# Who copies the turned tiles: ScalarE in place of VectorE, and a slot search in batches

## The chip, the core and the metric
The kernel runs on one core of a Trainium2 chip. The metric is the device time of one launch in microseconds (us), median over runs. TensorE multiplies and turns (transposes) tiles into PSUM, VectorE and ScalarE read PSUM and write SBUF, GpSimd issues the indirect DMAs (gather and scatter by row numbers), SyncE and ScalarE issue the plain DMAs. The engines run side by side, each in its own program order, and meet only at semaphores.

## The reference, cut to what matters
Images become patch tokens, text ids become rows of a table, and 12-head attention with its top 32 keys follows; all of that is unchanged here. The change is in the last step, a layer in which each of 2,176 tokens (32 sequences of 68) picks 4 of 128 matrices, twice: once to turn its 192 features into 128, once to turn 128 back into 192.

```
def topk_sparsify(weights, k):
    topk_vals, topk_idx = jax.lax.top_k(weights, k)
    ...
    sparse = sparse / (sparse.sum(axis=-1, keepdims=True) + 1e-08)
w_fk, _ = topk_sparsify(jax.nn.softmax(logits_fk, axis=-1), K)
w_rk, _ = topk_sparsify(jax.nn.softmax(logits_rk, axis=-1), K)
all_h = jnp.einsum('bsd,ndr->bsnr', x, neurons)
h = jnp.einsum('bsnr,bsn->bsr', all_h, weights)
all_out = jnp.einsum('bsr,nrd->bsnd', h, neurons)
out = jnp.einsum('bsnd,bsn->bsd', all_out, weights)
```

## The kernel before, in words
The tokens lie in NT = 17 tiles of 128, split into two parts: PARTS = tiles 0 to 8 and 9 to 16. The kernel doesn't form all 128 products of a token. It sends each token to the 4 matrices that it picked: every matrix has a block of HALVED = 64 slots in a part's slot table in DRAM, and tokens beyond 64 go to spill blocks behind the 128 own ones. Two matrices make one 128-slot tile, GROUP = 4 such tiles one group of 512 slots. Part 0 has 25 groups, part 1 has 24; 16 of each (PART_MAIN) hold the own blocks, the other 9 and 8 are spill groups, whose matrix is read from a table at run time. Part 0 takes its own groups first, part 1 its spill groups first (`first_order`).

The stages after the routing (which ends with `tiles_known`) are these.

- **Slot search** (`find_slots(r, i)` on VectorE, L1480 to L1507): for one tile i and one of the two products r, 12 instructions on 128x128 and 128x4 elements with a wait for the engine's own result between most of them give the 4 slot numbers of every token in `s_all`. `place` holds each token's position at each matrix, `base` where the matrix's spill begins. All 17 tiles of product 0 are searched first, in a row. Product 1's are searched one by one, each just before the tile's sum (`first_sums`).
- **Weights**: four small instructions on VectorE, after the 17 searches, then `weights_known`. `m_xT`, the buffer of turned tiles, lies over the first half of `place` and is cleared after that.
- **Send** (GpSimd, L692): four indirect DMAs for each tile write its rows to the slots `slots_x`, as soon as the tile's slots are known; `sent0` and `sent1` count them by part.
- **First product** (TensorE L1152 turns a slot tile, L1163 and L1166 multiply; 49 groups): SyncE loads groups of slot rows (`load_rows`, L456, 384 KB each, four buffers), TensorE turns them two tiles ahead (AHEAD = 2), VectorE copies the turned tile from PSUM to `m_halves` (L1534), TensorE multiplies, ScalarE copies the product to `m_yh` (L886) and stores a group (L889, 256 KB) to `slots_h`. SyncE's queue is in this order: the first 13 of 16 chunks of matrices, a wait for `weights_known` and `tiles_known`, the last 3 chunks (they lie over the routing's scratch), a wait for `sent0`, the row loads. The matrices of the second product (`load_r`, L462, 16 chunks of 768 KB) follow, chunk by chunk, as part 1's own groups free their room.
- **Gather, sum and spread**: when all of a part's first product is stored, GpSimd gathers for each tile the four rows of each token (`fetch(1, i)`, L700), VectorE sums them with the weights (`sum_back(1, i)`, L1559 and L1562), GpSimd scatters the sum to the 4 slots of the second product (`spread_sums`, L707). Its order is fetch(i), spread(i - 1), fetch(i + 1), with four gather buffers.
- **Second product** (L1201 turns, L1210 and L1212 multiply, VectorE copies at L1542, ScalarE keeps at L903): the same over `slots_g` and `slots_y`. It starts for a part when all of its sums are spread.
- **Output**: gathers from `slots_y` (L700 again), `sum_back(2, i)` with the residual (L1571), store (L487).

VectorE's order is written out by hand. It copies turned tiles group by group, and `beside` puts steps of other work between the groups: in the first product of part 1 the nine `first_sums` of part 0, in the second product of part 0 the eight of part 1, in the second product of part 1 the nine output sums of part 0. While VectorE searches and sums, no turned tile is copied.

## Time and profile before
| | |
|---|---|
| median of 3 runs | 1250.01 us (1247.91 to 1253.24) |
| profiled execution | 1248.79 us, span of its instructions 1247.0 us |
| mean granted clock of TensorE | 0.742 of full speed |
| busy in the span | TensorE 881.7 us, VectorE 753.1, GpSimd 529.8, ScalarE 329.2 |
| moved by DMA | 167.70 MB, mean 134 GB/s |

Times in the profile count from the span's start. The part before about 600 us is embedding, attention and routing, the part behind it the stages above. A row of the timeline gives start, length, engine, line, operation, output and input, how many instructions are merged, and in brackets the idle time before it with what ended it; "remote" is a releaser that the profile can't name. Each float32 matmul stands as two instructions.

### The profile page before, as it was taken

Reading aid. Unit: us, or ns where it says so; the run is one execution under the profiler, and the core shown is the slowest. Engines: PE = TensorE matmul, PEld = TensorE weight load, DVE = VectorE, ACT = ScalarE, POOL = GpSimd, SP = SyncE. Lnnn points to the kernel's source line nnn. Section 1 sums busy time; section 2 is a strip of 40 time slices with the busy share of each in tenths; the row PEclk is TensorE's granted clock in tenths of the full one; section 3 lists DMA queues with packets and bytes.
Section 4 is the critical chain, followed back from the end, with each engine's and each line's share of the span. In section 5 each row is a group of like instructions: output and inputs, shape, how many; then the busy total and the mean of one; then the engine's idle time right before and its main releaser. Section 6 shows DMA issues by size and latency. Waiting matters only on the chain.

```text
span 1247.0 us, 24432 instructions
## 1 busy us (share of the span) xinstructions
PE 881.7 (71%) x6616; PEld 750.0 (60%) x6616; DVE 753.1 (60%) x4773; ACT 329.2 (26%) x1042; POOL 529.8 (42%) x745
## 2 busy tenths in 40 slices
PE   4788988898989898667400099987778656757830
PEld 4788878888888787444200088987556333633630
DVE  1399999999999999444553444334445344424533
ACT  0234433333433343144200033211111222213410
POOL 3244444444544443245376500043443544454235
PEclk9778888787878655555555599987775676878975
DMA  5123332323233330086021555444785544447833
GB/s 189 33 69 110 141 110 89 109 89 109 90 109 111 113 113 25 19 208 162 7 79 67 169 196 188 149 126 126 256 318 205 182 146 151 140 154 229 272 127 95
DMA packets 81318, 167.70 MB, mean 134 GB/s; under 512 B 12944, under 2 KB 39376, under 8 KB 79536
## 3 DMA queue, kind: packets, MB, share of 16 engines
q1 hardware_dynamic: 55824, 111.18, 27.5%
q10 hardware_dynamic: 14112, 32.12, 7.4%
q0 software_dynamic: 11264, 23.09, 6.3%
q8 instruction: 42, 0.69, 0.2%
q14 instruction: 76, 0.62, 0.2%
HBM read 84.81 MB, written 81.53 MB: 133 GB/s over the span
## 4 chain that ended last, share of the span: by engine, by line
PE 36%; DVE 32%; issue 18%; POOL 5%; DMA 4%; another core or an unknown queue 2%; ACT 2%; DVEq 1%; SPq 0%; POOLq 0%; ACTq 0%
DVE work L1301 13%; DVE top L1295 9%; PE bank L1166 6%; PE bank L1163 5%; PE bank L1212 5%; PE bank L1152 4%; PE bank L1210 3%; POOL early L700 2%; PE bank L1201 2%; PE bank L1099 1%; PE bank L925 1%; PE bank L984 1%; PE bank L1006 1%; POOL slots_g L707 1%
## 5 line engine op out<-in xcount | busy, mean ns | idle before, releaser
L1301 DVE MATCH_REPLACE8 work<-top,work 102x68 f32<-102x68 f32 x1024 | 204.7, 212 | 0.0
L1534 DVE COPY place<-bank 96x256 f32<-96x256 f32 x196 | 74.5, 416 | 149.2 <-PE bank L1152 98.3
L1295 DVE MAX8 top<-work 102x8 f32<-102x68 f32 x1024 | 145.5, 213 | 3.2 <-ACT tru L767 1.9
L1152 PE MATMUL bank<-ident,early 128*96 128x128 f32 x392 | 73.4, 316 | 102.9 <-DMA early<-slots_x 101.2
L886 ACT ACTIVATE m_y<-bank 128x128 f32<-128x128 f32 x196 | 52.5, 278 | 304.2 <-PE bank L1166 207.9
L1542 DVE COPY place<-bank 128x128 f32<-128x128 f32 x196 | 47.5, 286 | 133.0 <-PE bank L1201 73.1
L707 POOL DMA_INDIRECT slots_g<-early,s_all x68 | 66.1, 973 | 138.8 <-DVE early L1562 123.2
L1152 PEld LDWEIGHTS bank<-ident,early 128*96 128x96 f32 x392 | 52.3, 175 | 118.3 <-issue 117.9
L700 POOL DMA_INDIRECT early<-slots_h,s_all x68 | 65.2, 959 | 122.9 <-DMA slots_h<-m_y 102.5
L925 PE MATMUL bank<-xa,early 128*96 128x144 f32 x512 | 102.0, 352 | 16.8 <-DVE early L1319 16.0
L903 ACT ACTIVATE m_y<-bank 128x192 f32<-128x192 f32 x196 | 61.1, 331 | 170.5 <-PE bank L1212 78.8
L1166 PE MATMUL bank<-f_all,place 96*64 96x128 f32 x1024 | 92.6, 324 | 15.0 <-issue 11.1
L925 PEld LDWEIGHTS bank<-xa,early 128*96 128x96 f32 x512 | 91.5, 200 | 18.2 <-issue 15.9
L1212 PE MATMUL bank<-r_all,place 128*64 128x192 f32 x512 | 70.3, 400 | 40.5 <-DVE place L1542 25.6
L700 POOL DMA_INDIRECT early<-slots_y,s_all x68 | 64.7, 952 | 68.8 <-DMA slots_y<-m_y 29.9
L1166 PEld LDWEIGHTS bank<-f_all,place 96*64 96x64 f32 x1024 | 71.9, 160 | 30.2 <-issue 18.2
L1006 PE MATMUL bank<-v,pT 68*68 68x17 f32 x768 | 75.9, 250 | 14.6 <-ACT pT L792 14.6
L1006 PEld LDWEIGHTS bank<-v,pT 68*68 68x68 f32 x768 | 74.0, 196 | 17.1 <-ACT pT L792 17.1
L692 POOL DMA_INDIRECT slots_x<-early,s_all x68 | 66.0, 970 | 40.8 <-DVE s_all L1506 20.6
L1163 PE MATMUL bank<-f_all,place 96*128 x544 | 73.5, 293 | 10.5 <-ACT m_y L886 4.3
L629 POOL TENSOR_TENSOR sc<-work,tru 102x544 f32<-102x544 f32 x32 | 42.7, 1333 | 90.0 <-ACT work L805 89.9
L1301 DVE MATCH_VALUE_LOAD work<-top,work 102x8 f32 x1024 | 80.2, 78 | 0.0
(179 smaller groups left out, 1815.9 us busy)
## 6 DMA issues: line engine op xcount, KB each, us to landing
early<-slots_x SPq DMA_DIRECT2D x49, 384.0 KB
slots_y<-m_y ACTq DMA_DIRECT2D x49, 384.0 KB
slots_h<-m_y ACTq DMA_DIRECT2D x49, 256.0 KB
early<-slots_g SPq DMA_DIRECT2D x49, 256.0 KB
f_all<-in_f_know SPq DMA_DIRECT2D x16, 768.0 KB, 5.6
r_all<-in_r_know SPq DMA_DIRECT2D x16, 768.0 KB
slots_x<-zero SPq DMA_DIRECT2D x28, 360.0 KB, 3.0
slots_x<-zero SPq DMA_DIRECT2D x28, 336.0 KB, 3.2
```

Of the source, the lines that this page charges most:

```text
L692: nc.gpsimd.indirect_dma_start(slots_x[part_of(i)], bass.IndirectOffsetOnAxis(s_all[:, 0, i, k:k + 1], 0), xn_all[:, i, :], None).then_inc ...
L700: nc.gpsimd.indirect_dma_start(g_in[:, i % DEPTH, k, 0:width], None, src, bass.IndirectOffsetOnAxis(s_all[:, r - 1, i, k:k + 1], 0)).then_ ...
L707: nc.gpsimd.indirect_dma_start(slots_g[part_of(i)], bass.IndirectOffsetOnAxis(s_all[:, 1, i, k:k + 1], 0), g_sum[:, i % DEPTH, 0:R], None) ...
L925: nc.tensor.matmul(half, wa[:, 4 * a + c, e * HALF:(e + 1) * HALF], xa[:, :, a:a + 2 * GRID - 1:2, c:c + 2 * GRID - 1:2], start=(a == 0 an ...
L1006: last = nc.tensor.matmul(ps_pt[0:S, head * (HD + 1):(head + 1) * (HD + 1)], pT[:, g, h * S:(h + 1) * S], v[:, par, head, :], start=True, ...
L1152: last = nc.tensor.transpose(turn_bank[t][0:HALF, c * P:(c + 1) * P], m_x[:, d, t, c:D:2], ident[:])
L1163: last = nc.tensor.matmul(bank[2 + t][:, 0:R], m_xT[0:HALF, t, c, h * P:(h + 1) * P], matrix[:, c * R:(c + 1) * R], start=(h == 0 and c == ...
L1166: last = nc.tensor.matmul(bank[2 + t][h * HALVED:(h + 1) * HALVED, 0:R], m_halves[0:HALF, t, c, h, :], matrix[:, c * R:(c + 1) * R], start ...
L1212: last = nc.tensor.matmul(bank[2 + t][h * HALVED:(h + 1) * HALVED, 0:D], m_halves[:, t, 0, h, :], matrix, start=True, stop=True)
L1295: last = nc.vector.max(top8[:, c, :], work[:, par, c, :])
L1301: last = nc.vector.match_replace(work[:, par, c, :], top8[:, c, :], work[:, par, c, :], TAKEN)
L1534: nc.vector.tensor_copy(m_halves[0:HALF, t], turn_bank[t][0:HALF, 0:2 * P].rearrange("p (c h s) -> p c h s", c=2, h=2)).then_inc(sem["m_xt ...
```

## The change
1. ScalarE copies the turned tiles in both products (`copy_turned`), two tiles ahead of the two that it keeps (`keep`). The wait for the whole of `m_out` between the products goes; each buffer is waited for when it is reused.
2. VectorE searches slots in BATCHES of 1, 2, 6 and 8 tiles: each instruction works on all tiles of the batch, but for the four comparisons of each tile, which stay single, with up to IN_FLIGHT = 8 of them not yet waited for (`Tally`). GpSimd waits for a tile's batch.
3. The weights are formed after the first two batches (3 tiles).
4. VectorE then does the rest of product 0's search, clears `m_xT`, does all of product 1's search, and after that only sums: 17 times `sum_back(1, i)`, 17 times `sum_back(2, i)`.

```
+BATCHES = ((0, 1), (1, 3), (3, 9), (9, NT))
+IN_FLIGHT = 8
...
+        s_f = sb("s_f", [P, IN_FLIGHT, K4])
+        s_i = sb("s_i", [P, 4, IN_FLIGHT, K4], I32)
         t_h = sb("t_h", [P, DEPTH, D])
...
+            def wait(self, lag=0):
+                self.eng.wait_ge(self.sem, self.count - lag)
...
-                pool.wait_ge(sem["slots_known0"], i + 1)
+                pool.wait_ge(sem["slots_known0"], 1 + [i < end for first, end in BATCHES].index(True))
...
+                pool.wait_ge(sem["slots_known1"], 1 + [i < end for first, end in BATCHES].index(True))
...
+            def copy_turned(r, j, t):
+
+                act.wait_ge(sem[f"m_turn{r}"], j * GROUP + t + 1)
+                if j >= 1:
+                    act.wait_ge(sem[f"m_mm{r}"], (j - 1) * GROUP + t + 1)
+                if r == 0:
+                    ins = nc.scalar.activation(m_halves[0:HALF, t], turn_bank[t][0:HALF, 0:2 * P].rearrange("p (c h s) -> p c h s", c=2, h=2), ACT.Copy)
+                else:
+                    ins = nc.scalar.activation(m_halves[:, t, 0], turn_bank[t][:, 0:P].rearrange("p (h s) -> p h s", h=2), ACT.Copy)
+                ins.then_inc(sem[f"m_xt{r}"], 1)
...
+            def keep(r, g, n, copies, width):
...
+                for t in range(0, GROUP, AHEAD):
+                    for ahead in range(t + AHEAD, t + 2 * AHEAD):
+                        if ahead < GROUP:
+                            copy_turned(r, j, ahead)
+                        elif n + 1 < PART_GROUPS[g]:
+                            copy_turned(r, j + 1, ahead - GROUP)
+                    if t == 0 and r * GROUPS + j >= DEPTH:
+                        act.wait_ge(sem[f"m_out{d}"], 16 * (in_turn(d, GROUPS) * r + j // DEPTH))
+                    for now in range(t, t + AHEAD):
+                        act.wait_ge(sem[f"m_mm{r}"], j * GROUP + now + 1)
+                        nc.scalar.activation(copies[:, d, now, :], bank[2 + now][:, 0:width], ACT.Copy).then_inc(sem[f"m_done{r}"], 1)
+                act.wait_ge(sem[f"m_done{r}"], (j + 1) * GROUP)
+
+            act.wait_ge(sem["halves_cleared"], 1)
             for g in range(2):
+                for t in range(AHEAD):
+                    copy_turned(0, FIRST_GROUP[g], t)
...
-            for d in range(DEPTH):
-                act.wait_ge(sem[f"m_out{d}"], 16 * in_turn(d, GROUPS))
...
+                    keep(0, g, n, m_yh, R)
...
+            act.wait_ge(sem["m_mm0"], GROUPS * GROUP)
...
-            slot_steps = [Steps(dve, f"slot_steps{r}", 6) for r in range(2)]
-
-            def find_slots(r, i):
-
-
-
-                st = slot_steps[r]
-                q, size = 2 * part_of(i) + r, HALVED
-                st.start(i)
-                st.done(nc.vector.scalar_tensor_tensor(s_over[:], place[:, r, i], float(size), base[:, q], ALU.is_ge, ALU.mult))
+            slot_steps = Tally(dve, "slot_steps")
+
+            def find_slots(r, n):
...
+                st = slot_steps
+                first, end = BATCHES[n]
+                size = end - first
+                here = place[:, r, first:end]
+                ids = idf[:, first:end, r]
+                starts = base[:, 2 * part_of(first) + r].unsqueeze(1).to_broadcast([P, size, NE])
+                st.done(nc.vector.scalar_tensor_tensor(s_hit[:, 0:size], here, float(HALVED), starts, ALU.is_ge, ALU.mult))
                 st.wait()
-                st.done(nc.vector.tensor_tensor(s_at[:], s_over[:], place[:, r, i], ALU.add))
+                st.done(nc.vector.tensor_tensor(here, s_hit[:, 0:size], here, ALU.add))
                 st.wait()
...
+                for m in range(size * K4):
+                    i, k = divmod(m, K4)
+                    if m >= IN_FLIGHT:
+                        st.wait(IN_FLIGHT - 1)
+                    st.done(nc.vector.scalar_tensor_tensor(s_hit[:, m % IN_FLIGHT], iota_e[:], ids[:, i, k:k + 1], here[:, i],
+                                                           ALU.is_equal, ALU.mult, accum_out=s_f[:, i, k:k + 1]))
                 st.wait()
...
-                nc.vector.tensor_tensor(s_all[:, r, i, :], s_i[:, 1], s_i[:, 3], ALU.add).then_inc(sem[f"slots_known{r}"], 1)
-                dve.wait_ge(sem[f"slots_known{r}"], i + 1)
-
-            for i in range(NT):
-                find_slots(0, i)
-
-
-            dve.wait_ge(sem["t_weights"], 2)
...
+                nc.vector.tensor_tensor(s_all[:, r, first:end], at[1], at[3], ALU.add).then_inc(sem[f"slots_known{r}"], 1)
+                dve.wait_ge(sem[f"slots_known{r}"], n + 1)
+
+            def spread_weights():
...
+            find_slots(0, 0)
+            find_slots(0, 1)
+            spread_weights()
+            for n in range(2, len(BATCHES)):
+                find_slots(0, n)
             nc.vector.memset(m_xT, 0.0).then_inc(sem["halves_cleared"], 1)
-            dve.wait_ge(sem["halves_cleared"], 1)
-
-            def turned_first(j):
-
-                for t in range(GROUP):
-                    dve.wait_ge(sem["m_turn0"], j * GROUP + t + 1)
...
-                    nc.vector.tensor_copy(m_halves[0:HALF, t], turn_bank[t][0:HALF, 0:2 * P].rearrange("p (c h s) -> p c h s", c=2, h=2)).then_inc(sem["m_xt0"], 1)
...
-                        dve.wait_ge(sem["m_mm1"], (j - 1) * GROUP + t + 1)
-                    nc.vector.tensor_copy(m_halves[:, t, 0], turn_bank[t][:, 0:P].rearrange("p (h s) -> p h s", h=2)).then_inc(sem["m_xt1"], 1)
+            for n in range(len(BATCHES)):
+                find_slots(1, n)
 
...
-            def first_sums(i):
-
-                find_slots(1, i)
+            for i in range(NT):
                 sum_back(1, i, R)
-
...
-                for n in range(PART_GROUPS[g]):
-                    turned(FIRST_GROUP[g] + n)
-                    while done < len(tiles) and (done + 1) * PART_GROUPS[g] <= (n + 1) * len(tiles):
-                        step(tiles[done])
...
+            for i in range(NT):
                 sum_back(2, i, D)
...
-            for n in range(PART_GROUPS[0]):
-                turned_first(n)
-            beside(turned_first, 1, range(*PARTS[0]), first_sums)
-            dve.wait_ge(sem["m_mm0"], GROUPS * GROUP)
-            beside(turned_second, 0, range(*PARTS[1]), first_sums)
-            beside(turned_second, 1, range(*PARTS[0]), output)
-            for i in range(*PARTS[1]):
-                output(i)
 
```

## Rows read from the trace of the kernel before
**Rows 1.** Busy time by stretch: us, busy (count) per engine, granted clock, DMA share, GB/s.
```profile
625.00:650.00 25.00, 0.00 (x0) 0.00 (x0) 14.83 (x93) 0.00 (x0) 18.97 (x20) 0.50 0.23 78
...
725.00:750.00 25.00, 25.00 (x299) 20.46 (x298) 11.26 (x30) 8.05 (x29) 0.00 (x0) 1.00 0.58 187
...
900.00:925.00 25.00, 18.92 (x168) 14.11 (x168) 13.61 (x57) 3.91 (x16) 12.72 (x13) 0.80 0.93 336
```

**Rows 2.** Waits after 600 us: total us, times, longest.
```profile
POOL slots_g L707 <- DVE early L1562: 123.2, 17, 11.7
...
DVE place L1534 <- remote: 48.4, 16, 7.5
...
ACT m_y L886 <- remote: 25.1, 9, 4.1
```

**Rows 3.** Timeline 600 to 730 us: start, length, engine, line, operation, idle before.
```profile
615.67 0.29 DVE L1488 SCALAR_TENSOR_TENSOR s_over<-place,base 128x128 f32<-128x128 f32 x1 [0.15 <-DVE tile_e L1475]
...
618.27 0.16 DVE L1506 CUSTOM_DVE_ANT_0 s_all<-s_i 128x8 uint16<-128x8 uint16 x1
...
619.30 1.19 POOL L692 DMA_INDIRECT slots_x<-early,s_all  x1 [13.11 <-DVE s_all L1506]
...
669.01 0.96 POOL L692 DMA_INDIRECT slots_x<-early,s_all  x1 [4.01 <-DVE s_all L1506]
...
702.34 0.30 DVE L1521 TENSOR_TENSOR weights<-e_all,e_sum 128x136 f32<-128x136 f32 x1
...
702.73 1.27 SPq L437 DMA_DIRECT2D f_all<-in_f_know  x3
...
712.00 0.96 POOL L692 DMA_INDIRECT slots_x<-early,s_all  x1 [0.30 <-issue]
...
716.23 1.93 PE L1152 MATMUL bank<-ident,early 128*96 128x128 f32 x8 [101.19 <-DMA early<-slots_x]
```

**Rows 4.** Chain that ended last: start, us, what.
```profile
773.01 1.79 PE bank L1163 x16
...
813.09 1.99 PE bank L1163 x16
...
1110.24 1.11 PE bank L1201 x4
...
1193.46 2.62 PE bank L1210 x16
```

**Rows 5.** Groups of instructions: count, busy us, mean ns, idle before.
```profile
L1534 DVE COPY place<-bank 96x256 f32<-96x256 f32 x196 | 74.5, 416 | 149.2 <-PE bank L1152 98.3
...
L886 ACT ACTIVATE m_y<-bank 128x128 f32<-128x128 f32 x196 | 52.5, 278 | 304.2 <-PE bank L1166 207.9
...
L861 ACT ACTIVATE place<-bank 128x256 f32<-128x256 f32 x12 | 4.4, 363 | 0.0
```

**Rows 6.** Timeline of TensorE, GpSimd and ScalarE in the second product.
```profile
974.80 1.09 PE L1201 MATMUL bank<-ident,early 128*128 128x128 f32 x4 [10.28 <-DMA early<-slots_g]
...
1105.00 0.96 POOL L707 DMA_INDIRECT slots_g<-early,s_all  x1 [0.30 <-issue]
...
1134.43 0.87 PE L1212 MATMUL bank<-r_all,place 128*64 128x192 f32 x8
...
1135.60 0.87 PE L1212 MATMUL bank<-r_all,place 128*64 128x192 f32 x8
...
1137.15 1.00 ACT L903 ACTIVATE m_y<-bank 128x192 f32<-128x192 f32 x4 [2.60 <-PE bank L1212]
...
1171.21 1.56 PE L1210 MATMUL bank<-r_all,place 128*128 x8 [1.59 <-ACT m_y L903]
```

**Rows 7.** Busy time from 637 to 665 us.
```profile
637.00:665.00 28.00, 0.00 (x0) 0.00 (x0) 5.97 (x37) 0.00 (x0) 21.29 (x23) 0.50 0.22 78
```

**Rows 8.** Timeline, first product of part 1: TensorE and GpSimd after idle time.
```profile
844.20 3.78 PE L1163 MATMUL bank<-f_all,place 96*128 x16 [3.01 <-DVE place L1534]
...
853.73 1.00 POOL L707 DMA_INDIRECT slots_g<-early,s_all  x1 [11.66 <-DVE early L1562]
```

More of the change, by code:

```diff
@@ L320, in wait, with __init__, done @@
                 self.eng.wait_ge(self.sem, self.base + self.at)
+        class Tally:
+            def __init__(self, eng, name):
+                self.eng, self.sem, self.count = eng, sem[name], 0
+            def done(self, ins):
+                ins.then_inc(self.sem, 1)
+                self.count += 1
+            def wait(self, lag=0):
+                self.eng.wait_ge(self.sem, self.count - lag)
         def logits_of(i):
@@ L908, in _ @@
-            for g in range(2):
-                for j in range(FIRST_GROUP[g], FIRST_GROUP[g] + PART_GROUPS[g]):
-                    keep_second(g, j)
+                    keep(0, g, n, m_yh, R)
+                    block_rows = first_order(g)[n]
+                    d = (FIRST_GROUP[g] + n) % DEPTH
+                    act.dma_start(slots_h[g][block_rows * GROUP * P:(block_rows + 1) * GROUP * P, :].rearrange("(p t) d -> p t d", p=P),
+                                  m_yh[:, d]).then_inc(sem[f"m_out{d}"], 16)
@@ new lines, in _ @@
+            act.wait_ge(sem["m_mm0"], GROUPS * GROUP)
+            for g in range(2):
+                for t in range(AHEAD):
+                    copy_turned(1, FIRST_GROUP[g], t)
+                for n in range(PART_GROUPS[g]):
+                    keep(1, g, n, m_y, D)
+                    d = (FIRST_GROUP[g] + n) % DEPTH
+                    act.dma_start(slots_y[g][n * GROUP * P:(n + 1) * GROUP * P, :].rearrange("(p t) d -> p t d", p=P),
+                                  m_y[:, d]).then_inc(sem[f"m_out{d}"], 16)
@@ L1489, in find_slots @@
                 st.wait()
-                st.done(nc.vector.tensor_tensor(s_at[:], s_over[:], place[:, r, i], ALU.add))
+                st.done(nc.vector.tensor_tensor(here, s_hit[:, 0:size], here, ALU.add))
                 st.wait()
-                for k in range(K4):
-                    last = nc.vector.scalar_tensor_tensor(s_hit[:, k, :], iota_e[:], idf[:, i, r, k:k + 1], s_at[:],
-                                                          ALU.is_equal, ALU.mult, accum_out=s_f[:, k:k + 1])
@@ L1495, in find_slots @@
-                st.done(last)
+                for m in range(size * K4):
[4 more added lines that the diff above has]
+                                                           ALU.is_equal, ALU.mult, accum_out=s_f[:, i, k:k + 1]))
                 st.wait()
-                st.done(nc.vector.scalar_tensor_tensor(s_i[:, 0], idf[:, i, r], float(size), s_f[:], ALU.mult, ALU.add))
+                at = [s_i[:, step, 0:size] for step in range(4)]
@@ L1503, in find_slots @@
+                nc.vector.tensor_scalar(at[2], at[0], 7, GROUP - 1, ALU.logical_shift_right, ALU.bitwise_and)
+                st.done(nc.vector.tensor_scalar(at[3], at[0], 9, 9, ALU.logical_shift_right, ALU.logical_shift_left))
                 st.wait()
-                st.done(nc.vector.tensor_tensor(s_i[:, 1], s_i[:, 1], s_i[:, 2], ALU.add))
+                st.done(nc.vector.tensor_tensor(at[1], at[1], at[2], ALU.add))
                 st.wait()
-                nc.vector.tensor_tensor(s_all[:, r, i, :], s_i[:, 1], s_i[:, 3], ALU.add).then_inc(sem[f"slots_known{r}"], 1)
@@ new lines, in find_slots @@
+                dve.wait_ge(sem[f"slots_known{r}"], n + 1)
+            def spread_weights():
+                dve.wait_ge(sem["t_weights"], 2)
+                nc.vector.tensor_reduce(e_sum[:], e_all[:], AX.X, ALU.add).then_inc(sem["t_weights"], 1)
+                dve.wait_ge(sem["t_exped"], NT)
+                dve.wait_ge(sem["t_weights"], 3)
+                nc.vector.scalar_tensor_tensor(z_all[:], z_all[:], 1e-8, e_sum[:], ALU.mult, ALU.add).then_inc(sem["t_weights"], 1)
+                dve.wait_ge(sem["t_weights"], 4)
+                nc.vector.reciprocal(e_sum[:], z_all[:]).then_inc(sem["t_weights"], 1)
+                dve.wait_ge(sem["t_weights"], 5)
+                nc.vector.tensor_tensor(weights[:], e_all[:], e_sum[:].unsqueeze(3).to_broadcast([P, NT, 2, K4]), ALU.mult).then_inc(sem["t_weights"], 1)
+                dve.wait_ge(sem["t_weights"], 6)
+                nc.vector.sem_inc(sem["weights_known"], 1)
```

54 lines of the change are left out of this document (4 added, 50 removed).

## The prediction, as it was put on record
> **What bounds the kernel now.** I read the stretches of 25 us first, to find where TensorE works and where not. From 625 to 650 us no engine but VectorE and GpSimd is busy; from 725 to 750 TensorE is busy throughout at a granted clock of 1.00 (the 2.4 GHz level); from 900 to 925 it is busy for 18.9 of 25 us at a clock of 0.80 on the mean, with the DMA engines at 0.93 and 336 GB/s [rows 1]. So the last half of the kernel is a chain of stages, and the change touches nothing before the first slot search at 615.7 us.
>
> The waits view names what holds the stages [rows 2]. GpSimd waits 123.2 us in 17 waits for VectorE's weighted sums before it can spread a tile. VectorE's copy of a turned tile waits 48.4 us in 16 waits, and ScalarE's keeping of a product 25.1 us in 9 waits, for a releaser that the profile can't name ("remote"). The timeline shows the largest single wait, 101.2 us of TensorE for the first slot rows [rows 3]: GpSimd's sends of part 0 are issued from 619.3 to 665.0 us, but SyncE loads the last matrices only at 702.7 and the first slot rows behind them, because the weights are formed after all 17 slot searches (last weight instruction 702.3 us). TensorE starts at 716.2. The slots of part 0 had been full for 50 us.
>
> Then the stages, by the chain and the timeline [rows 4, 6]: first product of part 0 716.2 to 813.1 (16 own groups in 56.8 us, 9 spill groups in 40.1 us, 4.45 each); first product of part 1 813.1 to 964.5 (974.80 less the 10.28 us of idle before it); second product starts at 974.8, its part 1 at 1110.2, its last matmul ends at 1196.1; the tail is 51 us, to the span's 1247.0.
>
> **The change, stage by stage.** *Copies move to ScalarE.* A copy of 96x256 takes 416 ns on VectorE; ScalarE's copy of the nearest shape, 128x256, takes 363 ns, and its own 128x128 copy 278 ns [rows 5]. A group then costs ScalarE at most 4 x 363 + 4 x 278 = 2.6 us and one DMA issue (SyncE's three matrix issues take 1.27 us, 0.42 each [rows 3]), so 3.0 us against 3.55 us that TensorE needs for an own group (56.8 / 16). It fits, so in the first product the move costs nothing as long as TensorE paces it; if the cover went, the loss would be at most a few tenths per group, under 10 us over 49 groups. In the second product the turned tile is 128x128 and the kept one 128x192, and TensorE's own group is 2 x 1.17 = 2.34 us [rows 6]. Back to back, ScalarE keeps four tiles of 128x192 in 1.00 us [rows 6], so eight copies and the issue are at most 2.0 + 0.42 = 2.4 us, level with TensorE; without overlap it is 4 x 278 [rows 5] and 4 x at least as much, 2.2 + 0.42 = 2.6 at the least, and some 0.5 us too slow if the wait for the last copy before the issue stands in the way: 16 us over 32 groups. I take nothing, the overlap being shown, and keep 16 us for the range. The page "ScalarE: Activation LUTs" of the Trainium skill (section "What ACT_TABLE_LOAD costs") gives 186 ns + 0.833 ns per element for such an instruction and an overlap of 93 ns between neighbours; that would be an estimate of 399 ns, 306 ns back to back, for 256 elements, so by it too ScalarE isn't the slower copier.
>
> *Slot search.* One tile takes 615.67 to 618.43, 2.8 us with its waits [rows 3]; GpSimd issued 36 sends from 619.30 to 669.01 - 4.01 = 665.0, 5.1 us per tile. Even unbatched the search keeps ahead, so batches gain only where waits are slow. That happens: between 637 and 665 us VectorE is busy for 6.0 of 28 us while GpSimd sends without a pause [rows 7], and GpSimd then loses 4.0 us before 669.0 [rows 3]. The batch of eight must be ready at 665; its work is between 3 us (nothing scales) and 22 us (everything does), started at about 634. I expect it at 665 to 670: sends end at 706 to 713 instead of 713.
>
> *Weights early.* Three tiles and four small instructions are done by 615.7 + 4 x 2.8 = 627. The three matrix loads then run beside the sends, and the row loads wait for the sends of part 0 alone, 665.0. From the last indirect issue to TensorE's first transpose the second product needed 1110.24 - 1105.96 = 4.3 us [rows 4, 6], so the first product can start at 669.3; the clearing of the halves comes after the batch of eight and can hold it to 680. I take 671 (before: 716.2), 45 us gained.
>
> *First product, part 0.* 97 us of TensorE, as before, but now the first 35 us lie beside sends. If handshakes were as slow there as VectorE's at 637 to 665 it would cost up to 20 us; between 0 and 20 I take 8. End 671 + 97 + 8 = 776 (813).
>
> *First product, part 1.* TensorE's own need is 8 x 4.45 + 16 x 3.55 = 92 us; it took 151 us, 59 lost. Losses: VectorE searching and summing between copies (removed), the short stops near the end of each run of eight indirect DMAs, in which copies wait for the unnamed releaser and TensorE for the copies (3.0 us in the one shown [rows 8]), and the lower clock after them. The second stays: 9 tiles x 3.0 = 27 us. For the third I take 11 us. Lower bound: row blocks, kept rows and the 12.6 MB of second matrices are 23 MB in the 16 own groups, with some 2.5 MB of gathers and spreads beside them 25.5 MB, at 336 GB/s 76 us in place of 57, so 112 us in all. Upper bound 151. I take 130: end 906 (964).
>
> *Second product, part 0.* It starts at 910, when rows are stored and the last matrices in. It ran 974.8 to 1110.2, 135.4 us, because spreading part 1 waited for VectorE (GpSimd: 11.7 us of idle before a spread [rows 8]). GpSimd alone needs 8 x 10.2 + 4 + 4.3 = 90 us. TensorE needs 16 x 2.34 + 9 x 3.11 = 65 us (8 spill groups in 24.9 us [rows 6]), plus 8 x 3.0 of stops, plus 10 for the clock: 99. I take 100: end 1010 (1110).
>
> *Second product, part 1.* 62 us of TensorE; it took 86. The gathers of part 0's outputs now come without pauses, 9 x 5.1 = 46 us, since VectorE sums at once. Between 67 (no stops) and 98 I take 84: end 1094 (1196). *Tail* unchanged, 51 us: 1145. The profiled run is 1.8 us above its span and 1.2 us under the median of 1250.0, so **1148 us**, 102 less (8%).
>
> **Rivals.** *Free handshakes.* The stops might be a matter of VectorE beside a busy GpSimd alone; with the copies on ScalarE TensorE would no longer feel them. The "GPSIMD Engine Reference" of the Trainium skill (section 1, Specifications) says the SBUF interfaces are shared with VectorE and contend with instructions of two SBUF inputs; by that rule the copies, which read PSUM, would be no contender and the sums would, off TensorE's path. Its price follows from the terms above, without any stop: 670 + 97 + 112 + 4 + 90 + 67 + 51 + 3 = 1094 us, and 1110 with ScalarE's shortage of 16 us. For it: VectorE's long idle stretch with nothing else running [rows 7]. Against it: ScalarE's keeping, which touches neither VectorE nor GpSimd, waits for the unnamed releaser too [rows 2].
>
> *Starved handshakes.* GpSimd's pauses are what lets the others recover; without pauses VectorE ran at 6.0/28 = 0.21 of its time [rows 7]. If only half of that took hold: stops double in both products (17 tiles x 3 = 51 us more) and the part 0 sends cost their 20: 1148 + 63 = 1211 us.
>
> *No gain or slower.* The same starvation in full: TensorE at a rate of 0.15 in all of GpSimd's unbroken runs. 19 us of work done by 710 (16 before the stops set in, as they did 18 us after the first send, and 3); the other 78 by 788; GpSimd's 91 us hold 14, the remaining 78 end at 957; from 961 its 85 us hold 13, the remaining 52 end at 1098; 46 us hold 7, the remaining 55 end at 1199; with tail and surround 1253 us: no change at a rate of 0.15, slower below it. Against it: GpSimd's runs depend on VectorE's sums, which would starve too and make it pause; that is the wait before a spread in [rows 8].
>
> *The change doesn't bite:* if the weights' early forming left the start at 716, 45 us come back: 1193.
>
> **How the numbers follow.** Forecast case (1120 to 1180) 0.45; free handshakes (under 1120) 0.20; heavier stops or a late start (1180 to 1244) 0.27; no change 0.03; slower 0.05. The range 1105 to 1210 leaves out about 0.2; the likeliest case's own is 1120 to 1180. A measurement of this kernel tells 0.5% (6 us) from no change: faster 0.92, same 0.03, slower 0.05.
>
> **What would show it.** The first transposes at 669 to 680 us; sends ending by 713; ScalarE keeping TensorE's pace of 1.7 us per pair in the own groups of part 0; no VectorE wait before a spread above 5 us; the second product's start near 910 and its part 1 near 1010; a tail of 51 us. The prediction is wrong if TensorE's stops beside indirect DMAs grow or vanish: then the part 1 stages are off in the same direction, all three. It is wrong too if ScalarE comes to be what TensorE waits for at the group ends of the second product, where a store issue stands between two copies.

## The result, and the profile after
| | before | after |
|---|---|---|
| median | 1251.62 us (4 runs, 1247.91 to 1267.62) | 1313.93 us (4 runs, 1311.11 to 1319.29) |
| ratio | | **1.0513**, 95% interval 1.0461 to 1.0565 |
| span, granted clock | 1247.0 us, 0.742 | 1309.3 us, 0.727 |
| busy in the span: TensorE, VectorE, GpSimd, ScalarE | 881.7, 753.1, 529.8, 329.2 us | 853.7, 606.3, 533.6, 426.8 us |

The change makes the kernel 5.1% slower, where I forecast 8% faster. The ratio leaves out one slow run of the kernel before (1267.62 us). VectorE lost 147 us of work and ScalarE gained 98, as meant.

Windows of the changed kernel; columns: length, busy us (instructions) of TensorE, its weight loads, VectorE, ScalarE, GpSimd, then granted clock, DMA share, GB/s:
```profile
637.00:665.00 28.00, 0.00 (x0) 0.00 (x0) 26.46 (x155) 0.00 (x0) 21.95 (x20) 0.50 0.21 74
676.00:712.00 36.00, 8.98 (x48) 6.14 (x48) 6.14 (x29) 1.78 (x5) 27.26 (x29) 0.50 0.34 123
725.00:750.00 25.00, 25.00 (x276) 20.19 (x273) 0.00 (x0) 15.69 (x54) 0.00 (x0) 0.90 0.56 179
850.00:875.00 25.00, 1.11 (x3) 0.33 (x2) 2.73 (x8) 0.28 (x1) 18.98 (x20) 0.50 0.17 50
900.00:925.00 25.00, 8.61 (x39) 7.67 (x40) 0.70 (x2) 3.67 (x13) 6.06 (x7) 0.51 0.13 45
```
Read the first engine column against GpSimd's. Where GpSimd rests (725 to 750) TensorE works throughout, as before [rows 1]. From 850 to 875 GpSimd issues indirect DMAs without a pause, and TensorE issues 3 matmuls and ScalarE one copy in 25 us, while the DMA engines are busy for 0.17 of the time: traffic is not what they wait for. VectorE is another matter: from 637 to 665, beside sends as unbroken as before, its search in batches does 155 instructions in 26.5 of 28 us, where the kernel before did 37 in 6.0 [rows 7].

Timeline of the changed kernel:
```profile
676.85 1.92 PE L1181 MATMUL bank<-ident,early 128*96 128x128 f32 x8 [60.04 <-DMA early<-slots_x]
...
688.50 0.37 PE L1181 MATMUL bank<-ident,early 128*96 128x128 f32 x1 [2.42 <-issue]
...
691.31 0.37 PE L1181 MATMUL bank<-ident,early 128*96 128x128 f32 x1 [2.44 <-issue]
...
718.37 2.03 PE L1195 MATMUL bank<-f_all,place 96*64 96x128 f32 x16 [20.41 <-ACT place L899]
...
816.53 0.99 POOL L713 DMA_INDIRECT early<-slots_h,s_all  x1 [104.75 <-DMA slots_h<-m_y]
...
841.24 0.37 PE L1192 MATMUL bank<-f_all,place 96*128 x1 [2.41 <-issue]
...
1002.62 0.63 PE L1230 MATMUL bank<-ident,early 128*128 128x128 f32 x4 [0.97 <-DMA early<-slots_g]
...
1157.34 0.97 POOL L713 DMA_INDIRECT early<-slots_y,s_all  x1 [69.78 <-DMA slots_y<-m_y]
```
The first product does start at 676.9, 39 us earlier than before [rows 3], and then does nothing of note until the sends end (the last is issued at 710.8): it runs from 718.4, so its part 0 ends where it ended before. GpSimd's run for part 0 lasts from 816.5 to 907.9, in which TensorE, after 7 us at full pace, issues mostly single matmuls at distances that are multiples of 0.70 us, with "issue" and no engine named before them. Only then does part 1 of the product go on, so that the second product starts at 1002.6 (974.8 before [rows 6]). There the same happens again.

Waits of the changed kernel after 600 us: total us, times, longest:
```profile
ACT m_y L918 <- remote: 175.9, 18, 21.4
...
POOL early L713 <- DMA slots_y<-m_y: 114.3, 2, 69.8
...
PE bank L1241 <- ACT place L901: 84.5, 9, 24.4
```
The wait for the unnamed releaser was 25.1 us in 9 waits [rows 2] and is 175.9 in 18. GpSimd's 123.2 us of waits for VectorE's sums [rows 2] are gone: it works in one stretch, and then waits for the product that it held up.

Groups of the changed kernel: count, busy us, mean ns, idle before:
```profile
L899 ACT ACTIVATE place<-bank 96x256 f32<-96x256 f32 x196 | 64.7, 376 | 113.3 <-issue 72.3 <-PE bank L1181 24.3 <-remote 12.1
L918 ACT ACTIVATE m_y<-bank 128x128 f32<-128x128 f32 x196 | 53.9, 277 | 163.9 <-remote 112.5 <-PE bank L1192 30.8 <-PE bank L1195 17.3
```
ScalarE's copy of a turned tile takes 376 ns, less than VectorE's 416 [rows 5].

### The profile page after: what moved, and what is told of

The parts are those of the page before. It is cut to its first block, busy times and chain, and to the rows that moved or that the text cites. A ratio compares the mean times of both kernels' runs of the same rounds, so it can differ in the third digit from the quotient of the medians.

```text
span 1309.3 us, 24240 instructions
## 1 busy us (share of the span) xinstructions
PE 853.7 (65%) x6616; PEld 730.5 (56%) x6616; DVE 606.3 (46%) x4173; ACT 426.8 (33%) x1434; POOL 533.6 (41%) x745
## 4 chain that ended last, share of the span: by engine, by line
PE 34%; DVE 24%; another core or an unknown queue 16%; issue 16%; POOL 4%; ACT 3%; DMA 3%; DVEq 0%; ACTq 0%; POOLq 0%; SPq 0%
DVE work L1330 11%; DVE top L1324 8%; PE bank L1195 5%; PE bank L1192 5%; PE bank L1241 4%; PE bank L1181 4%; PE bank L1239 3%; POOL early L713 2%; PE bank L1230 2%; PE bank L954 2%; PE bank L1013 2%; PE bank L1035 1%; PE bank L1128 1%; PE bank L989 1%
## 5 line engine op out<-in xcount | busy, mean ns | idle before, releaser
L1580 DVE TENSOR_SCALAR early<-early,weights 128x128 f32<-128x128 f32 (+1 forms) x34 | 10.5, 308 | 473.0 <-DMA early<-slots_h,s_all 336.9
L918 ACT ACTIVATE m_y<-bank 128x128 f32<-128x128 f32 (+1 forms) x392 | 115.9, 306 | 278.6 <-remote 175.9
L1241 PE MATMUL bank<-r_all,place 128*64 128x192 f32 x512 | 65.4, 380 | 111.2 <-ACT place L901 84.5
L1192 PEld LDWEIGHTS bank<-f_all,place 96*128 96x128 f32 x544 | 69.9, 206 | 67.2 <-issue 67.2
L954 PEld LDWEIGHTS bank<-xa,early 128*96 128x96 f32 x512 | 96.3, 211 | 18.9 <-issue 16.2
L1241 PEld LDWEIGHTS bank<-r_all,place 128*64 128x64 f32 x512 | 33.8, 151 | 130.8 <-ACT place L901 91.2
L899 ACT ACTIVATE place<-bank 96x256 f32<-96x256 f32 x196 | 64.7, 376 | 113.3 <-issue 72.3
L1195 PE MATMUL bank<-f_all,place 96*64 96x128 f32 x1024 | 80.7, 300 | 22.1 <-ACT place L899 20.4
L705 POOL DMA_INDIRECT slots_x<-early,s_all x68 | 70.3, 1034 | 33.5 <-issue 20.4
L1195 PEld LDWEIGHTS bank<-f_all,place 96*64 96x64 f32 x1024 | 63.7, 147 | 34.2 <-ACT place L899 22.7
```

What stands on the lines that cost most here:

```text
L705: nc.gpsimd.indirect_dma_start(slots_x[part_of(i)], bass.IndirectOffsetOnAxis(s_all[:, 0, i, k:k + 1], 0), xn_all[:, i, :], None).then_inc ...
L899: ins = nc.scalar.activation(m_halves[0:HALF, t], turn_bank[t][0:HALF, 0:2 * P].rearrange("p (c h s) -> p c h s", c=2, h=2), ACT.Copy)
L918: nc.scalar.activation(copies[:, d, now, :], bank[2 + now][:, 0:width], ACT.Copy).then_inc(sem[f"m_done{r}"], 1)
L954: nc.tensor.matmul(half, wa[:, 4 * a + c, e * HALF:(e + 1) * HALF], xa[:, :, a:a + 2 * GRID - 1:2, c:c + 2 * GRID - 1:2], start=(a == 0 an ...
L1192: last = nc.tensor.matmul(bank[2 + t][:, 0:R], m_xT[0:HALF, t, c, h * P:(h + 1) * P], matrix[:, c * R:(c + 1) * R], start=(h == 0 and c == ...
L1195: last = nc.tensor.matmul(bank[2 + t][h * HALVED:(h + 1) * HALVED, 0:R], m_halves[0:HALF, t, c, h, :], matrix[:, c * R:(c + 1) * R], start ...
```

## The experiments
Three theories. **Starved issue:** GpSimd's unbroken runs of indirect DMAs keep TensorE and ScalarE from issuing; the pauses that VectorE's copies imposed on GpSimd had let them work. **Late handshakes:** only signals between engines are late. **Scalar pace:** ScalarE is too slow in the order of its list. All line edits are against the changed kernel unless said otherwise. Runs of one comparison share their runs of the kernel before.

**e1_probe: streams that wait for nothing.**
```
+            pe.wait_ge(sem["summed2"], PARTS[1][0] + 1)
+            for m in range(500):
+                nc.tensor.matmul(bank[2][0:HALVED, 0:HALVED], ident[:, 0:HALVED], ident[:, 0:HALVED], start=True, stop=True)
...
+            act.wait_ge(sem["summed2"], PARTS[1][0] + 1)
+            for m in range(120):
+                nc.scalar.activation(probe_a[:, m:m + 1], ident[:, m:m + 1], ACT.Copy)
```


> The changed kernel, and behind the second product, from the tenth output sum on, TensorE issues 500 matmuls of 64x64 and ScalarE 120 copies of one column, none of which waits for anything, while GpSimd gathers the outputs of part 1 in its last 35 us or so. Starved issue (GpSimd's unbroken indirect DMAs keep the other engines from issuing at all): TensorE and ScalarE start near one instruction in 0.70 us a few us into the run, as in the stalled stretches, and go to 0.05 us or less and some 0.1 us for one when GpSimd ends. Late handshakes (only semaphores between engines are slow): both streams run at full rate from the first instruction, within some 25 and 20 us, beside GpSimd. Scalar pace (ScalarE is just too slow in the order of its list) says nothing of this and expects full rate too. The run as a whole stays within 2% of 1314 us, unless the starved streams end it.

Measured: 1364.55 us (one run). Timeline of this kernel, first TensorE, then ScalarE (a matmul stands as two instructions; GpSimd gathers from 1260.9 to about 1301):
```profile
1269.59 5.29 PE L1274 MATMUL bank<-ident 128*64 128x64 f32 x45 [11.62 <-DVE early L1601]
...
1276.04 0.27 PE L1274 MATMUL bank<-ident 128*64 128x64 f32 x1 [1.15 <-issue]
...
1282.34 0.27 PE L1274 MATMUL bank<-ident 128*64 128x64 f32 x1 [3.13 <-issue]
...
1305.45 56.76 PE L1274 MATMUL bank<-ident 128*64 128x64 f32 x939 [1.14 <-issue]
...
1269.48 2.15 ACT L943 ACTIVATE probe_a<-ident 128x1 f32<-128x1 f32 x22 [11.14 <-DVE early L1601]
...
1276.02 0.20 ACT L943 ACTIVATE probe_a<-ident 128x1 f32<-128x1 f32 x1 [1.12 <-issue]
...
1305.43 2.71 ACT L943 ACTIVATE probe_a<-ident 128x1 f32<-128x1 f32 x28 [0.50 <-issue]
```
Both streams start at full rate, stall within 2 to 5 us, crawl at one instruction in 0.7 to 3.5 us, and are at full rate again at the same moment, 1305.4, a few us after GpSimd's last gather. Nothing in them waits for a semaphore. Late handshakes falls as the whole story: issue itself is starved.

**e2_memset and e12_direct: GpSimd busy in another way; e11_narrow: a quarter of the bytes.** In all three the first product's gathers and scatters are replaced (of each only the gather's line is shown; `busy` is a memset of 128x256), so the second product works on other data.
```
e2:  +                        busy()
     +                        nc.gpsimd.memset(g_in[:, i % DEPTH, k, 0:width], 0.0).then_inc(sem[f"held{i % DEPTH}"], 16)
e12: +                        nc.gpsimd.dma_start(g_in[:, i % DEPTH, k, 0:width], src[(i % 8 * K4 + k) * P:(i % 8 * K4 + k + 1) * P, :]).then_inc(sem[f"held{i % DEPTH}"], 16)
e11: +                    nc.gpsimd.indirect_dma_start(g_in[:, i % DEPTH, k, 0:width if r == 2 else NARROW], None, src if r == 2 else src.rearrange("n (a d) -> (n a) d", d=NARROW),
```


> The changed kernel with the 136 gathers and scatters of the first product's results left out (second product works on zeros, output is the residual and gathers of zeros): in the place of each GpSimd clears two SBUF tiles, with the same waits before them and the same order, so GpSimd is busy but issues no DMA. Starved issue or late handshakes by indirect DMAs: TensorE no longer stops; part 1 of the first product takes 92 to 112 us in place of 190, part 0 of the second under 80 us in place of 155, and the time falls to some 1110 to 1180. If GpSimd's being busy were what stops the others, or if ScalarE's pace were it, the stops stay as long as GpSimd's runs are, and both parts stay over 130 us.

> The changed kernel, with the 136 gathers and scatters of the first product as direct DMAs of the same shape from GpSimd (fixed rows, so the results are other ones). If what starves the others is that GpSimd itself writes a descriptor for every row, the stops go with the indirection, and as direct issues are short the time falls to 1050 to 1150. If GpSimd's direct DMAs are made in the same way, 1290 or above.

> The changed kernel, but the gathers and scatters of the first product move 32 of the 128 columns of each row (a quarter of the bytes, other rows than the right ones, the rest of the sums left as it was), with the same number of DMAs and of rows. If the bytes in flight do it, the stops shrink to a quarter and the time falls under 1200. If it is the number of rows or of DMAs issued, stops and time stay: 1290 to 1320.

Measured, one run each: 1134.28, 1145.12 and 1315.21 us. Windows of the kernel with memsets, of that with direct DMAs, of that with narrow rows:
```profile
820.00:900.00 80.00, 77.79 (x789) 68.39 (x789) 16.93 (x29) 46.09 (x158) 21.04 (x122) 0.94 0.79 294
```
```profile
820.00:868.00 48.00, 48.00 (x473) 45.58 (x471) 12.14 (x36) 27.06 (x94) 38.39 (x72) 1.00 0.81 260
```
```profile
850.00:875.00 25.00, 1.59 (x5) 0.67 (x4) 4.08 (x12) 0.28 (x1) 19.21 (x20) 0.50 0.07 13
```
With as many direct DMAs of the same shape TensorE works 48.0 of 48 us beside 260 GB/s; with indirect ones of a quarter of the bytes it works 1.59 of 25 beside 13 GB/s. So neither bytes nor GpSimd's being busy does it, but the indirect DMAs' issue. For the second point the direct DMAs count for more than the memsets: they keep GpSimd busy for 38.4 of 48 us, as the gathers do (69.7 of 91.4), the memsets only for 21.0 of 80. ScalarE copies in all of these, so scalar pace falls too.

**e3_paced and e4_vector: the pauses back, one way and the other.**
```
e3: +                pace(1, i)
    +                if groups > 0:
    +                    pool.wait_ge(sem[f"m_mm{product}"], groups * GROUP)
```
In e3 `pace(1, i)` stands ahead of a tile's scatters and `pace(2, i)` ahead of its output gathers. In e4 the copies, ScalarE's keeping and `beside` are as before the change; batches and early weights stay.


> The changed kernel with one thing more: before GpSimd scatters a tile's sums (and before it gathers an output tile of part 0) it waits until TensorE has done the share of the product beside it that VectorE's order gave before, so its runs of indirect DMAs are 8 long again with pauses between. Starved issue: TensorE gets the pauses; part 1 of the first product takes 115 to 130 us again in place of 190, and the whole comes out well below the changed kernel, 1190 to 1250. Scalar pace: nothing of the loss comes back, 1300 to 1330, since waiting more on GpSimd cannot make ScalarE faster.

> The changed kernel, but VectorE copies the turned tiles again, with the order that spread its sums between the groups; batches and early weights stay, product 1's search stands before the first copy (9 tiles) and between the products (8). Starved issue: VectorE's copies hold its sums back and so give GpSimd its pauses, part 1 of the first product is back under 155 us and part 0 of the second under 140, the start does not come before 710 to 720 as the sends starve it; 1215 to 1255, level with before or up to 3% below. If early start, batches or traffic were the cost, it stays at 1290 or above.

Measured: 1238.77 us, ratio to before 0.987 (0.981 to 0.993), and 1229.00 us, 0.980 (0.973 to 0.988). Both give back more than the whole loss. Timeline of the paced kernel, one run of eight DMAs:
```profile
884.47 1.00 POOL L737 DMA_INDIRECT slots_g<-early,s_all  x1 [7.65 <-PE bank L1212]
...
888.11 1.14 PE L1212 MATMUL bank<-f_all,place 96*64 96x128 f32 x16
...
893.44 1.13 PE L1212 MATMUL bank<-f_all,place 96*64 96x128 f32 x8 [3.57 <-issue]
...
897.48 2.03 PE L1212 MATMUL bank<-f_all,place 96*64 96x128 f32 x16
...
900.47 2.03 PE L1212 MATMUL bank<-f_all,place 96*64 96x128 f32 x16
```
The run begins at 884.5. TensorE keeps 1.69 us a pair for 5 us, stops for 3.6 us, and then does 16 instructions in 2.03 us instead of 1.14. A window from 885 to 890 has a granted clock of 1.00 (the 2.4 GHz level), one from 894 to 902 of 0.50 (the 1.2 GHz level). So a stop costs its own length and, at 3.0 us a pair instead of 1.7 until the clock is back, some 3 us more. A run of four DMAs, 5.1 us, would be over before such a stop sets in.

**e5 to e10: rests.** `rest()` stands behind 4 DMAs or behind each, in the sends of part 1, the first product's gathers and scatters, and the output gathers of part 0 (e5: in those sends alone).
```
+            def rest():
+                for _ in range(REST):
+                    idle.wait()
+                    idle.done(nc.gpsimd.memset(rest_tile[:], 0.0))
```
The memset is of 128x256 elements, in e10 of 128x8.


> The changed kernel with GpSimd resting (six small memsets, waiting for each; an estimated 2.5 us) behind every 4 sends of part 1, and nowhere else. Starved issue: the first product starts at 677 us as before, but now really gets the time between the sends, and its part 0 ends 25 to 40 us earlier than 813; nothing else changes, so 1275 to 1290 in place of 1314. If 4 sends in a row starve it already, or a rest of 2.5 us gives nothing back, the part ends at 805 or later and the time is 1305 to 1325.

> The changed kernel with a rest of three memsets (an estimated 1.3 us) behind every 4 indirect DMAs: sends of part 1, all gathers and scatters of the first product, output gathers of part 0. Starved issue with stops that set in 5 to 8 us into a run: runs of 4 last 5 us, so if 1.3 us is pause enough there are no stops: part 1 of the first product about 115 us, part 0 of the second about 107, the whole 1130 to 1160. If the pause is too short to clear what has built up, stops stay and it ends between 1180 and 1290. Scalar pace: no gain, since the rests only add GpSimd time, 1314 plus 20 to 60.

> As the run with rests of three memsets, but six (an estimated 2.6 us). Starved issue: no stops at all; GpSimd sets the pace, 18 runs of 7.7 us beside part 1 of the first product (140 us), 16 beside part 0 of the second (125), then some 70 us and the tail of 51: 1165 to 1185. If the shorter rest is already enough, this is 30 to 40 us slower than that one; if not, it is the faster of the two. Scalar pace: slower than 1314.

> The same mean rate of DMAs as with six memsets behind 4, spread evenly: two memsets (an estimated 0.8 us) behind every single indirect DMA. If a backlog builds up in a run and drains in a pause (so that the mean rate counts), this equals the run with six behind 4 within 2%, or beats it for having fewer stops. If the length of a pause counts (the others need some us without any indirect DMA), TensorE still stops and this one is at least 3% slower than it.

> One memset of 0.35 us behind every indirect DMA where two stood (one DMA in some 1.5 us in place of 1.9). If that is still pause enough TensorE runs free of stops as it did with two (part 1 of the first product in 94 us) and GpSimd, which set the pace there, saves 0.35 us on each of 136 DMAs, 48 us less the part that TensorE then takes back: 1105 to 1130. If stops come back below 1.9 us for a DMA, the first product's part 1 takes over 105 us and the time is 1145 to 1200. If the spacing only matters as a mean rate, three memsets behind 4 (one DMA in 1.54 us) has the same rate, and this one comes out at 1161 too.

> A memset of 8 columns (0.1 us) behind every indirect DMA, one DMA in some 1.3 us, as in the changed kernel itself: it tells whether the length of the pause does it, or merely that another kind of instruction stands between two DMAs. Length: stops as in the changed kernel, 1270 to 1320. Any instruction between: like the run with one full memset or better, 1080 to 1130.

| run | memsets | median | ratio to before (95%) |
|---|---|---|---|
| e5 | 6 behind 4, sends alone | 1291.87 | 1.029 (1.025 to 1.034) |
| e6 | 3 behind 4 | 1161.46 | 0.925 (0.921 to 0.929) |
| e7 | 6 behind 4 | 1184.49 | 0.941 (0.933 to 0.948) |
| e8 | 2 behind each | 1155.99 | 0.922 (0.917 to 0.926) |
| e9 | 1 behind each | 1215.08 | 0.968 (0.962 to 0.974) |
| e10 | 8 columns behind each | 1309.43 | 1.044 (1.037 to 1.051) |

Windows of the kernel with two memsets behind each, then of that with one:
```profile
676.00:712.00 36.00, 33.47 (x369) 27.17 (x369) 5.57 (x40) 21.23 (x74) 31.82 (x59) 0.90 0.80 245
820.00:873.00 53.00, 49.07 (x536) 39.50 (x536) 5.21 (x16) 30.64 (x106) 45.12 (x86) 0.90 1.02 403
```
```profile
676.00:712.00 36.00, 16.82 (x93) 11.61 (x94) 6.60 (x37) 4.20 (x13) 31.98 (x50) 0.50 0.32 111
820.00:900.00 80.00, 61.60 (x398) 53.96 (x396) 9.82 (x28) 22.39 (x75) 71.07 (x110) 0.73 0.45 139
```
Leaving GpSimd more to do takes up to 12% off the changed kernel (1156 against 1314). A rest of two memsets, 0.70 us, behind each DMA frees TensorE (33.5 of 36 us beside sends, where it had 9.0). One of 0.33 us frees it in part: 16.8 us there, at half the clock and with 93 instructions instead of 369, and a ratio of 0.968. One of 0.12 us changes little (1.044, the changed kernel 1.051). My forecast for e9 (1105 to 1130, with stops 1145 to 1200) was too low in either case, and e5 came out 2 us above its range. The spacing follows no single rule that I tried. At one DMA in 1.5 us the bundled rest is better (e6 0.925, e9 0.968), which speaks for the length of the pause; at one in 1.8 us the spread rest is (e8 0.922, e7 0.941), which speaks against it. e5 shows the early start's worth once sends leave room for it, 22 us of the 40 lost there.

**e13 to e18: a condition without starvation.** In the comparisons of the last six runs the kernel before took 1123 us (17 runs, 1115 to 1138) and 1126 us (13 runs, 1117 to 1138), not 1250 to 1257. So they are only compared among themselves. e13 and e18 are one kernel (two memsets behind each send and output gather, three behind 4 in between), e14 has VectorE's copies (e4) with e8's rests, e15 is e8 with `spread_weights()` behind all searches of product 0, e16 is the kernel before with e8's rests, e17 the changed kernel itself.

> The changed kernel with two memsets behind every single DMA in the sends of part 1 and the output gathers of part 0, and three behind 4 in the gathers and scatters between. The best of the two earlier kernels in each stage, if the stages' losses only add: of the run with three behind 4 (1161) it takes away the 32 us that part 0 of the first product lost beside sends, and some 15 us beside the output gathers: 1110 to 1130. If the stages' losses are not separate, it stays at 1145 to 1160.

> The kernel with VectorE's copies and its order of sums between them, with the two memsets behind every DMA that gave 1156 with ScalarE's copies. It prices the move of the copies with the starvation gone. If the move is a gain (VectorE's sums, about 10 us a part, no longer stand between copies, and GpSimd no longer waits for them): 1175 to 1215. If ScalarE's copies cost time themselves (scalar pace), this one is faster than 1156. If neither, both are level within 1%.

> The changed kernel with two memsets behind every DMA (1156), but the weights are formed after all searches of product 0, so the matrices and the first slot rows come later, at some 676 us instead of 626. It prices the early weights with the starvation gone: the start of the first product moves from 680 to 685 to 705, as the batches are searched by 670, so 1160 to 1180. In my sum the early weights alone were worth 45 us; that would be 1200.

> The kernel before, with nothing of the change, and two memsets behind every DMA in the same places. If the rests alone are the gain, it comes near 1160. If the change's parts and the rests are both needed: the stops of 3 us and the low clock behind them go (some 25 us in each product), VectorE's order and the late start stay: 1195 to 1235.

> The changed kernel itself, once more, because in the last comparison the kernel before took 1123 us in all its runs, not 1250 (a chip or a moment without the starvation). If the kernel before again takes 1250 here, this one takes 1305 to 1325. If it takes 1123, starvation is absent and my sum without stops holds, the free handshakes rival: 1040 to 1100, faster than before by 2 to 7%, and the profile shows TensorE at full pace beside unbroken runs of indirect DMAs.

> The changed kernel with mixed rests, once more. With the kernel before at 1250: 1108 to 1135 if the rests take all starvation away, since rests that do their work leave nothing that depends on it; a ratio to before near 0.89. With the kernel before at 1123: 1118 again, a ratio of 0.99 to 1.00, and slower than the changed kernel without rests, to which the rests add only GpSimd's time.

| run | median | ratio to before (95%) |
|---|---|---|
| e17 changed kernel | 1087.19 | **0.965** (0.957 to 0.972) |
| e18, e13 mixed rests | 1116.34, 1117.72 | 0.992 (0.988 to 0.997), 0.995 (0.991 to 0.999) |
| e14 VectorE's copies, rests | 1164.58 | 1.040 (1.034 to 1.046) |
| e15 late weights, rests | 1163.05 | 1.037 (1.031 to 1.043) |
| e16 before, rests | 1161.74 | 1.036 (1.030 to 1.043) |

The window of [rows 7] in e16, whose code up to there is that of the kernel before:
```profile
637.00:665.00 28.00, 0.00 (x0) 0.00 (x0) 25.61 (x159) 0.00 (x0) 21.30 (x23) 0.50 0.23 79
```
GpSimd sends exactly as before (21.3 us busy, 23 instructions), and VectorE is busy for 25.6 us of the 28 instead of 6.0. The same instructions of GpSimd slow the same search in one condition and not in the other. Windows of e17, the program of the runs after:
```profile
676.00:712.00 36.00, 36.00 (x312) 28.08 (x309) 0.03 (x1) 18.83 (x62) 25.25 (x27) 0.69 0.67 219
850.00:875.00 25.00, 20.28 (x208) 16.04 (x208) 2.79 (x8) 12.16 (x42) 17.84 (x19) 0.86 1.03 410
```
Its timeline, the starts of the stages:
```profile
782.10 0.99 POOL L713 DMA_INDIRECT early<-slots_h,s_all  x1 [72.92 <-DMA slots_h<-m_y]
...
883.51 1.09 PE L1230 MATMUL bank<-ident,early 128*128 128x128 f32 x4 [5.09 <-DMA early<-slots_g]
...
968.42 1.11 PE L1230 MATMUL bank<-ident,early 128*128 128x128 f32 x4 [15.12 <-DMA early<-slots_g]
...
1036.89 0.95 POOL L713 DMA_INDIRECT early<-slots_y,s_all  x1 [27.15 <-DMA slots_y<-m_y]
```
36.0 of 36 us beside the sends (9.0 in the starved runs), 20.3 of 25 beside the first run (1.1). Without starvation the change is worth 3.5%, and rests only cost: GpSimd comes to set the pace. In e14, e15 and e16 it waits for VectorE's sums for 0.8, 0 and 3.3 us in all, and the second product starts at 917.6, 920.7 and 914.3 us. That is why the three are level and price neither the copies nor the weights.

## Why the prediction was wrong
**The step that failed** is the dismissal of the rival *no gain or slower*: "GpSimd's runs depend on VectorE's sums, which would starve too and make it pause". They did not starve enough. In 850 to 875 VectorE issues 8 instructions in 2.73 us of work, and a sum has four: it needs so few instructions per tile that GpSimd never waits for it. What had made GpSimd pause was VectorE's copies and searches between the sums, which the change takes away; e3 and e4 put pauses back by two ways that have nothing else in common, and both come out under the kernel before. I had the rate that would make it slower, TensorE's work below 0.15 of its full pace. The busy share is above that (8.98 of 36 us beside the sends, 19.7 of 91.4 beside the first run), but at half the clock. Counted in instructions at the full pace of the rows, 48, 104 and 80 beside the sends and the first two runs are worth 4, 12 and 9 us in 35, 91 and 81, so 0.12 to 0.13. That rival's sum gave 1253 us at 0.15; the trace is behind it by 26 us at the end of part 0 (814 against 788) and by 16, 14 and 4 us in the three stages after it. Of the 26, 15 are work beside the sends: I let TensorE do 19 us of it there, 16 of them before the stops set in, and it did 4, as they set in 7 us behind its first instruction.

Point by point, with the stages as starts in the span:

| | predicted | after, starved | e17, not starved |
|---|---|---|---|
| first product starts | 671 | 676.9, at full pace from 718.4 | 673 |
| its part 0 ends | 776 | 814 | 779 |
| second product starts | 910 | 1002.6 | 883.5 |
| its part 1 starts | 1010 | 1154 | 968.4 |
| its last matmul ends | 1094 | 1258.6 | 1033.9 |
| span | 1145 | 1309.3 | 1084.6 |

*Early weights, 45 us:* right as a start and empty as a gain in the starved runs, because part 0, for which I had 97 + 8 us, took 137 (676.9 to 814): the 8 us for slow handshakes beside the sends were 40. (In e17 it took 106.) The start is hardly owed to the weights either. Without starvation TensorE starts at 677.0 us with the weights behind all searches (e15), at 673.0 with them early (e17), and at 679.7 with the search and the weights of the kernel before (e16): 4 to 7 us, not 45. I had put down to the order of the code what the slow search of [rows 7] had done. With starvation present the changed kernel's search isn't slow (26.5 of 28 us), so there the batches may have brought the start forward; no run takes them and the weights apart.

*The stops, 3.0 us for a tile:* the row was right, its extrapolation wrong. It was the price of runs of eight with a pause between; e3's timeline shows the stop beginning 5 us into a run. Without pauses it doesn't repeat per tile, it lasts: ScalarE's longest wait is 21.4 us, TensorE's longest idle 27.5 (to 884.5).

*Free handshakes (1094, chance 0.20):* what e17 measures, 1087. Its terms come near: part 0 of the first product 106 us (97), part 1 99 (112), part 0 of the second 85 (90), its part 1 65.5 (67), tail 50.7 (51), with two errors that partly cancel, so that the closeness of the sum is in part luck. As a gain it doesn't hold, since without starvation the kernel before takes 1126, not 1250. But its reason was wrong: TensorE does feel indirect DMAs with the copies on ScalarE (after), and where it doesn't, VectorE's searches don't either (e16). The rule of the Trainium skill's "GPSIMD Engine Reference" (section 1, Specifications) on shared SBUF interfaces explains neither: e1's stalls are on TensorE, and e2's memsets of SBUF stop nobody.

*ScalarE as copier:* right. 376 ns a copy, 1.7 us a pair kept in part 0 and, in e17, 65.5 us for part 1 of the second product.

**The mechanism,** as far as shown: where starvation is present and indirect DMAs follow each other on GpSimd within about 0.5 us, the issue of TensorE and ScalarE falls to one instruction in 0.70 us or a multiple, after a start at full rate. Pauses of 0.86 us (two memsets) behind each prevent most of it; pauses of 1.5 behind four do so beside the gathers (45.4 of 53 us of TensorE in e6) but not beside the sends (22.6 of 36, at a clock of 0.50). That the descriptors which GpSimd writes for every row are what holds up the others' supply of instructions fits e11 and e12, but was only argued; so was that the few us of full rate come from instructions already fetched. Not explained: VectorE's search in the changed kernel runs beside unbroken sends at full rate for some 45 us, in the same comparisons in which TensorE is held up after 7.

**Open:** why the starvation was absent in the last comparisons. One chip number served both the first four experiments, with it, and e13 to e16, without it, half an hour later, so it is not a property of the number. The mixed rests were not measured with starvation present, nor the copies and the weights one by one in a kernel without rests.

## What to carry to other kernels
Before an engine is relieved, ask whose pauses its work was making: here VectorE's copies and searches were what broke up GpSimd's runs of indirect DMAs, and without them two products and the gathers beside them went one after the other. A stop that a trace shows once per burst is a function of the burst's length, not a price per item; break such runs with pauses, and measure how long they must be (0.7 us of memsets behind each was enough here, 0.33 only in part). Compare only with a kernel before that ran beside it: the same two programs came out 5.1% slower and 3.5% faster in two conditions, and rests won 8% in the one, where in the other the kernel without them was the fastest of all (1087 against 1116).

## What the runs showed of the hardware
- Unbroken indirect DMAs on GpSimd can starve TensorE and ScalarE of issue, without any semaphore: single matmuls at multiples of 0.70 us, 3 in 25 us, at 50 GB/s of traffic (after) or 13 (e11). As many direct DMAs of the same shape from GpSimd leave TensorE at 48.0 of 48 us (e12).
- VectorE's search was slowed so in the kernel before (5.97 of 28 us, [rows 7]) and not in the changed one (26.46 of 28 in the same window).
- TensorE keeps its full rate for 5 to 7 us before it is held up: from the start of a run (e3), from its own first instruction 9 us into a run (e1) or 56 us into one (after). ScalarE keeps it for 2 us (e1). Both have it again 4 us behind the last gather (e1). TensorE's granted clock is 0.50 for some 8 us behind a stop (e3).
- It can be absent: [rows 7] against the same window in e16, 5.97 and 25.61 us.
